# The batch loop of a selective-scan kernel's second stage: three written-out copies against one hardware loop

## What is computed

```python
xn = layernorm(x)
out = x + mamba(xn) + ffn(xn)

# mamba, cut down
hs, gate = split(Win @ xn)                  # 1024 channels each
hs = silu(causal_conv4(hs) + bconv)
dt_in, Bm, Cm = split(Wx @ hs)              # 128, 16, 16
dt = softplus(Wdt @ dt_in + bdt)
h_t = exp(A * dt_t) * h_(t-1) + dt_t * Bm_t * hs_t    # 16 states per channel
y_t = sum_n(h_t[n] * Cm_t[n])
mamba = Wout @ ((y + hs * D) * silu(gate))
# ffn, operands rounded to fp8
ffn = W_linear @ (gelu(W_g0 @ xn) * (W_g1 @ xn))
```

## Time and profile before

| | |
|---|---|
| time, median of 3 runs | 1151.44 us (1149.67 to 1152.3) |
| the profiled execution's own time | 1151.44 us |
| its span in the profile | 1149.7 us |
| mean granted TensorE clock | 0.922 of full speed |
| busy: DVE, POOL, PE, ACT | 91%, 81%, 81%, 68% |
| block B's first scan starts | near 242 us |

### The profile page before, as it was taken

The page is one execution under the profiler, slowest core; times in us unless marked ns, Lnnn a source line. Parts: engine busy times, 40 slices in busy tenths (PEclk is TensorE's granted clock), DMA queues, the critical chain, the costliest instruction groups (busy, mean ns, idle before and its releaser), DMA issues.

```text
span 1149.7 us, 14675 instructions
## 1 busy us (share of the span) xinstructions
PE 932.7 (81%) x4304; PEld 573.4 (50%) x4304; DVE 1041.4 (91%) x1237; ACT 784.8 (68%) x1117; POOL 926.6 (81%) x751
## 2 busy tenths in 40 slices
PE   4979798747777798888887988887988788787988
PEld 3746465424444455555444555554545545454554
DVE  6958778579999999999999999999999999999994
ACT  3878887647777755767785557777846577787551
POOL 5333424389999999989999999999989989999991
PEclk9999999967998899899988998899889899989899
DMA  7566767983111217522212183321213922212100
GB/s 279 204 240 219 266 220 265 341 329 116 51 55 38 83 37 224 206 87 72 80 51 83 43 288 137 116 74 56 83 37 102 326 81 69 74 46 74 37 1 37
DMA packets 53158, 150.24 MB, mean 131 GB/s; under 512 B 5728, under 2 KB 14048, under 8 KB 50016
## 3 DMA queue, kind: packets, MB, share of 16 engines
q1 hardware_dynamic: 53088, 149.41, 37.7%
HBM read 111.37 MB, written 38.01 MB: 130 GB/s over the span
## 4 chain that ended last, share of the span: by engine, by line
POOL 52%; DVE 13%; issue 7%; PE 5%; ACT 0%; DVEq 0%; POOLq 0%
POOL dbu L928 38%; POOL hp L939 14%; DVE da L985 3%; DVE prod L954 3%; DVE hp L985 3%; PE mm L1026 2%; DVE gate_bf L1000 2%; DVE act L1003 2%; PE yT L1104 1%; PE mm L1083 1%; PE da L1026 1%; PE mm L1074 1%; ACT da L887 0%; DVE y L960 0%; ACT gate_bf L895 0%
## 5 line engine op out<-in xcount | busy, mean ns | idle before, releaser
L887 ACT ACTIVATE da<-unit,neg_a 128x512 f32<-128x512 f32 x512 | 340.2, 685 | 263.1 <-DVE prod L954 256.7
L928 POOL TENSOR_TENSOR dbu<-unit,b_head 128x512 f32<-128x512 f32 x384 | 478.0, 1280 | 3.5 <-POOLq L99 3.5
L985 DVE TENSOR_TENSOR_SCAN da<-da,dbu 128x512 f32<-128x512 f32 x352 | 418.3, 1217 | 7.7 <-POOL dbu L928 6.5
L1104 PE MATMUL yT<-ident,prod 128*128 128x128 f32 x1408 | 238.2, 298 | 150.4 <-DVE prod L954 149.8
L1104 PEld LDWEIGHTS yT<-ident,prod 128*128 128x128 f32 x1408 | 174.8, 151 | 282.1 <-DVE prod L954 242.1
L939 POOL TENSOR_TENSOR hp<-hp,c_head 128x512 f32<-128x512 f32 x128 | 163.6, 1278 | 59.0 <-DVE act L1003 45.9
L985 DVE TENSOR_TENSOR_SCAN hp<-da,dbu 128x512 f32<-128x512 f32 x160 | 193.4, 1209 | 7.9 <-ACT da L887 7.9
L954 DVE TENSOR_TENSOR prod<-da,c_head 128x512 f32<-128x512 f32 x256 | 171.3, 669 | 0.0
L928 POOL TENSOR_TENSOR dbu<-unit,b_all 128x512 f32<-128x512 f32 x128 | 160.4, 1280 | 0.0
L1062 PE MATMUL mm<-xn_b,w_sb 128*128 128x512 fp8e4 x512 | 151.6, 432 | 4.4 <-ACT gate_bf L895 3.3
L1074 PE MATMUL mm<-xnT_b,wgate 128*128 128x512 f32 x256 | 127.9, 597 | 1.8 <-ACT gate_bf L895 1.7
(11 more groups left out here) (107 smaller groups left out, 1248.2 us busy)
## 6 DMA issues: line engine op xcount, KB each, us to landing
unit<-unit_d SPq DMA_DIRECT2D x32, 768.0 KB, 4.3
unit_d<-dt_du SPq DMA_DIRECT2D x32, 512.0 KB, 2.8
wf<-in_wffn SPq DMA_DIRECT2D x12, 1024.0 KB, 5.9
c_head<-bc_d SPq DMA_DIRECT2D x24, 512.0 KB, 5.0
b_head<-bc_d SPq DMA_DIRECT2D x18, 512.0 KB, 5.2
unit_d<-hsd SPq DMA_DIRECT2D x32, 256.0 KB, 3.9
w_sb<-w_d SPq DMA_DIRECT2D x64, 128.0 KB, 3.3
wgate<-in_win_gate SPq DMA_DIRECT2D x32, 256.0 KB, 2.7
```

The source lines that it names most:

```text
L887: nc.scalar.activation(da[n % SLOTS][:, :], unit[:, k % 2, 0, :], ACT.Exp, scale=neg_a[:, k, n:n + 1]).then_inc(da_ready, 1)
L928: nc.gpsimd.tensor_tensor(dbu[:, n % DBUS, :], unit[:, k % 2, 1, :], b_all[n // NS][:, n % NS, :], ALU.mult).then_inc(dbu_ready, 1)
L985: nc.vector.tensor_tensor_scan(state, da[n % SLOTS][:, :], dbu[:, n % DBUS, :], 0.0, ALU.mult, ALU.add).then_inc(scanned, 1)
L1104: ins = nc.tensor.matmul(yT[k % 2][:, t * P:(t + 1) * P], product[:, t * P:(t + 1) * P], ident[:, :], start=False, stop=last, is_transpose ...
```

## The change

The Python loop over the batches in `run_units` and in SP's own order becomes a hardware loop with three passes. `b` is then a register's value in the body, so wait values and DRAM addresses that depend on it are computed by register operations. Units 0 to 3 of batch 0 ahead of the loop and units 4 to 7 of the last batch behind it stay written out. `last_batch` can't compare a register's value, so it now asks whether `b` is a Python number outside the opening.

```diff
@@ run_units (scalar, gpsimd, vector and tensor queues) @@
             for k in range(HT):
                 body(0, k, True)
-            for b in range(B - 1):
+            with eng.Fori(0, B - 1) as b:
                 for k in range(HT, KU):
                     body(b, k, False)
                 for k in range(HT):
@@ SP: loads @@
             def loads(b, k, opening):
                 u = b * KU + k
-                last_batch = b == B - 1
+                last_batch = isinstance(b, int) and not opening
                 if not (opening and k == 0) and not (last_batch and k == KU - 1):
@@ SP: order of the loads @@
             for k in range(HT):
                 loads(0, k, True)
-            for b in range(B - 1):
+            with sp.Fori(0, B - 1) as b:
                 for k in range(HT, KU):
                     loads(b, k, False)
                 for k in range(HT):
```

## The result

In nine runs each, the kernel before took 1149.67 us (median; 1146.63 to 1153.02) and the changed one 1154.91 us (1153.32 to 1158.79), 5.2 us more. The measured ratio is 1.0058, with a 95% interval of 1.0042 to 1.0075, so 4.8 to 8.6 us: slower. (It is not the quotient of these two medians, which is 1.0046; all 34 executions of the changed kernel on record have a median of 1155.64 us.) The profiled execution of the changed kernel took 1155.15 us for a span of 1153.4 us.

What follows compares the result with a forecast made beforehand. DVE sets the time, busy 215.5 of 221.1 us per batch, POOL 206.8. The profiled 1151.44 us plus two taken branches of 1.9 us (3.8), register operations and table loads 0, gave 1155.2 us; range 1150.8 to 1161.0.

Steps and rivals of the forecast that it cites:

- Slower, by one pause per taken branch: Block B's loop: engines stand for one instruction block load at each of two taken branches, 3.8 us in all; likeliest case, 50%.
- One L of 3.0 us for all engines: L is the time of one instruction block load at a taken branch: 3.0 us taken, 1.6 and 4.3 as ends.
- ACT sets the cost, L - 1.1 = 1.9 us: Start of unit 4: ACT has 1.1 us covered; the rest of its stall delays DVE through `da` 1, 1.9 us per branch.
- DVE, L - 1.35, lies beside it: First scan of unit 4: DVE has 1.35 us covered; its 1.65 us stall runs parallel to ACT's and adds nothing.
- POOL hidden: Start of unit 4: POOL's first product ends 0.3 us after the scan's old start, less than ACT's delay, so adds nothing.
- PE and SP hidden: At the branch: PE's late transposes still finish before DVE reads them, SP's next load is needed 27.6 us later; no cost.
- Register operations 0: Looped units: computing wait values and addresses is hidden by sequencers running ahead, 0 us; exposed as a rival, 7%, up to 30.7 us.
- Table loads 0: Loop head on ACT: both ways in carry the same preload, so 0 us; an added load as a rival, 15%, 3.8 us.
- Instruction loads fall by less than half: Code moved by DMA after 200 us: falls, but by less than half, if the bodies are reloaded.
- The faster rival: Unit 5, DVE's wait for PE's L1026: a shifted pause or clock could give back 4.1 us, 1147.3 us; chance 6%.

Runs made afterwards that it cites:

- hint: The changed kernel with a branch hint at the head of every looped body, announcing the branch at its end: 1151.62 us, ratio 0.9994 to the kernel before.
- act_only: The kernel before with block B's batches looped on ACT's queue alone, the other queues written out: 1156.49 us, ratio 1.0040.
- pe_sp_only: The changed kernel with only PE's and SP's queues looped, the other three written out again: 1151.28 us, ratio 1.0001 to the kernel before.
- before_again: The kernel before, unchanged, run once more to see its own spread: 1151.21 us, ratio 0.9999.

## Why the prediction was right, and where its steps were not

**Slower, by one pause per taken branch: shown.** The pauses lie at the two taken branches and nowhere else, and a prefetched branch takes them away with the time (hint). The forecast was 1155.2 us, the median measured 1154.91. That agreement is partly luck: 3.8 us were added to 1151.44, while the median of before beside it was 1149.67. The cost was 5.2 us by the medians, 5.4 us in the profile and 6.7 us by the ratio, 1.4 to 1.8 times the forecast of 3.8.

**One L of 3.0 us for all engines: mis-sized.** It was 2.5 to 2.7 us on ACT and POOL, 3.3 to 3.7 on PE, 4.1 on DVE, and 0.3 on SP, which stood for no block at all. The prediction kept 4.3 us as an upper end because the unit load shares the DMA engines, but then gave every engine the middle. Which engine's branch comes behind that load could have been read from the trace of before. ACT's sequencer stands at unit 4 at 571.7 us and DVE's at 574.8, and SP issues in between:

```profile
L748 SPq DMA_DIRECT2D unit<-unit_d x1: 328/328/328, 572.6 to 572.6; - x1
```

**ACT sets the cost, L - 1.1 = 1.9 us; DVE, L - 1.35, lies beside it: the order failed.** DVE idles 2.23 us per branch. ACT's chain alone costs 1.76 and 1.90 us (act_only), so the 1.9 us came out, but by two misses that nearly offset each other (luck): a pause of 2.5 instead of 3.0 us, and a cover (what the engine has in hand when its sequencer stops) of 0.7 instead of 1.1. DVE's cover is 4.10 - 2.23 = 1.87 us instead of 1.35. With one L for both, ACT would have ruled as forecast; with its own 4.1 us DVE is the longer. The step that failed is that DVE's stall "is smaller, so it adds nothing"; that the longest is paid and not the sum was right. Against the untaken third pass units 3 + 4 are 58.04 - 55.69 = 2.35 us longer. 2.23 us of it is the idle time and 0.40 us the longer L1000, and the second scan starts 1.83 us after the first and not 2.19 us, since `da` is there: 2.27 us.

**POOL hidden: half right.** Its products were ready in time. What was overlooked is where its work moves to: into L1000 and L1003. Alone it costs 1.4 to 1.5 us per branch. In the full change DVE is late as well, and 0.40 and 0.51 us of it are left (L1000 takes 1.35 and 1.46 us).

**PE and SP hidden: right at this place** (pe_sp_only), because no result of PE is due for several states. At unit 7 it would not hold for PE.

**Register operations 0:** 0.1 us at each of a few units, 0.3 us in the third pass, so some 0.8 us for the loop (hint). It is a term missing from the sum, and too small to be measured by itself. **Table loads 0:** right, ACT's count is the same.

**Instruction loads fall by less than half: wrong, they rose** from 64 to 93 packets, 0.77 to 1.06 MB. Each body is loaded anew on every pass, as its 70 packets in hint show, and 23 more come with the branches that are not announced.

**The faster rival's mechanism is real but isn't the change's:** the wait of unit 5 differs between executions of one program (before_again). It takes 4.0 us off the difference between the profiles of before and after, and block B's later start, 2.5 us, adds to it. Both scatter from one execution to the next. With 5.4 us for the passes and 0.2 us less behind the last unit's start that makes the 3.7 us between the spans, 1149.7 and 1153.4 us.

## What to carry to other kernels

In this kernel a hardware loop cost each engine with a long body (327 instructions per pass and more) a late block of code at every taken branch: 2.5 to 3.0 us on ACT, POOL and DVE, 3.3 us or more on PE, and some 4 us when a large DMA had just been issued. The engine with 248 paid 0.3 us. Little more than the longest chain is paid, so put the branch where no engine's result is due soon, keep big loads behind it, and judge each engine by what it does in the next few microseconds and not by its share of busy time. If the loop can announce its branch, do that first: it removed all of the cost here but 0.8 us.

## What the runs showed that was not expected

- A block of instructions comes only after the 768 KB that were issued ahead of it: DVE's pause is 3.8 to 4.6 us behind that load and 2.8 to 3.0 us without it.
- One engine's delay can cost another time without a wait in the trace: POOL's products under L1000 and L1003 stretch them from 0.95 to 1.48 and from 0.96 to 1.80 us.
- Where PE's result is due at once, a pause of PE is followed by a second cost: the granted clock is 0.50 in the 3.4 us behind it, and a piece of 3.60 us takes 5.39 us.
- The looped kernel moves more code than the written-out one, 93 packets against 64, and 70 with the hint. With the hint the pause falls to between 0.2 and 0.6 us.
